# Shifted-window attention: the next pair's queries, keys and values projected ahead of a slot's transposes instead of behind its attention products

## The chip, the cores and the metric

One core of a Trainium2 chip runs the whole program. The metric is the device time of one execution in microseconds (us), lower is better. Engines are named as the profile names them: PE is TensorE (PEld its weight loads), ACT is ScalarE, DVE is VectorE, POOL is GpSimd.

## The reference

An input of 64 x 8192 goes through a convolution front end and then four residual blocks over 64 sequences of 128 positions with 64 channels. The change lies in the first block, attention inside windows of 128 positions. Here the sequence is exactly one window long, so it is plain attention with a position bias:

```python
h = h + _L0_attn_ref(_layernorm(h, axis=-1), qkv_weight, qkv_bias, proj_weight, proj_bias, bias_table)

qkv = xw @ qkv_weight.T + qkv_bias                 # 8 heads of 8 channels
attn = jnp.einsum('whqd,whkd->whqk', q * scale, k)
attn = attn + jnp.transpose(rpb, (2, 0, 1))[None]  # bias by relative position
attn = jax.nn.softmax(attn, axis=-1)
out = jnp.einsum('whqk,whkd->wqhd', attn, v).reshape(Bb * nW, WINDOW, C)
out = out @ proj_weight.T + proj_bias
```

All data is float32.

## The kernel before, in words

Each engine runs its own instruction stream, written out by hand, and semaphores join the streams. The stage of interest is the second (`stage2_pe`, `stage2_act`, `stage2_dve`, `stage2_pool`, lines 598 to 877). It works on pairs of sequences: two sequences of 64 channels fill the 128 partitions, which makes 32 pairs. A pair takes four **turns** (the code calls one `u`), each for four of its sixteen head-and-sequence combinations, so that one turn fills one PSUM bank of 128 x 512.

`pipelined` (line 580) calls `slot(i, t)` on every engine, with `i` from 0 to 16 and `t` from 0 to 7. Eight slots are two pairs: `l = t // 4` is the pair, `u = t % 4` the turn. Iterations 1 to 14 are a hardware loop on PE, ACT and DVE (on POOL from 2), the others are unrolled, and 16 is the tail. I call slot 4 of an iteration "slot 4", and a turn by the slot in which its scores are read.

A turn travels through the slots like this:

- Slot u = 0 of a pair: PE computes the scores of all four turns (L686, `scores`).
- Slot t: DVE adds the bias, and takes the extreme of each row (L836, four instructions), after which the scores are in SBUF.
- Slot t+1: ACT takes the exponential with a running sum (L787, four instructions of two records each).
- Slot t+2: DVE takes the reciprocal of the sums (L825), and POOL scales the weights (L620, `normed`).
- Slot t+3: PE transposes the weights into bank 4 (L738, four instructions). DVE (L845, even turns) or ACT (L792, odd turns) copies bank 4 to SBUF. There is one bank for it, so the next turn's transposes wait for that copy.
- Slot t+4: PE multiplies them by the values (L704, `attended`).

Around this, once for each pair:

- u = 0: PE transposes the next pair's normalised rows (L668, `rows`), ACT copies them (L767), PE projects the finished pair (L716, `project`) and DVE adds this to h (L858), which counts `a_h_r` up.
- u = 1: PE computes queries, keys and values of the next pair (L674, L675, L676, `qkv`), ACT copies the queries (L771) and DVE the keys (L818). `qkv` waits for the copied rows (L767) and for `a_h_r` of the projection in the slot just before (L858), since keys and projection share bank 3.
- u = 2: POOL spreads the keys over heads (L614, `spread`), which the next scores wait for.
- u = 3: PE runs `unread` (L691), one matmul of 128 x 512 whose result nobody reads, DVE copies the heads' outputs (L852), ACT the values (L777), and POOL prepares the next rows (L602, L606).
- Once in an iteration, at slot 5, DVE also sums and centres four finished sequences for the next layer norm (L275, L277).

The order within PE's slot is what the change touches. It was: scores, unread, the transposes L738, attended (not at u = 0), then `qkv` at u = 1.

Of the kernel before, what the change touches and what calls it, by code (L numbers as in the profile page):

```python
# [59 lines left out]
def build(nc, xp, consts, out):  # L60
# [8 lines left out]
    def c(name, a=0, b=None):  # L69

        o, w = ON[name]
        return cst[:, o + a:o + (w if b is None else b)]
# [263 lines left out]
    def bank(b):  # L336
        return T(b // 4, b % 4)
# [229 lines left out]
    N2 = NP // 2  # L567

    def back(i, t, d):

        return (i, t - d) if t >= d else (i - 1, t - d + 8)

    def i_is(i, k):
        return isinstance(i, int) and i == k

    def exists(i, d, last=N2 - 1):

        return not isinstance(i, int) or 0 <= i + d <= last

    def pipelined(engine, slot, ahead=1):  # L580

        for i in range(ahead):
            for t in range(8):
                slot(i, t)
        with engine.Fori(ahead, N2 - 1) as i:
            for t in range(8):
                slot(i, t)
        for t in range(8):
            slot(N2 - 1, t)
        for t in range(8):  # L590
            slot(N2, t)
# [3 lines left out]
    def scores_bank(t):  # L595
        return bank(SBANK[t % 4])
# [65 lines left out]
    def stage2_pe(pe, start=None):  # L662
        def rows(i, l):
            pe.wait_ge(a_xs_r, i * 2 + (l + 1))

            if l or exists(i, -1):
                pe.wait_ge(a_v_r, i * 2 + l)
            nc.tensor.transpose(bank(2)[:, 0:128], xs[l], eye).then_inc(a_t_r, 1)  # L668

        def qkv(i, l):  # L670
            pe.wait_ge(a_xT_r, i * 2 + (l + 1))

            pe.wait_ge(a_h_r, i * 2 + (l + 1))
            nc.tensor.matmul(bank(2)[:, 128:256], c("a_q"), xT[l], start=True, stop=True)  # L674
            nc.tensor.matmul(bank(3)[:, 0:128], c("a_k"), xT[l], start=True, stop=True)  # L675
            nc.tensor.matmul(bank(2)[:, 256:384], xT[l], c("a_v"), start=True, stop=True).then_inc(a_qkv_r, 1)  # L676

        def scores(i, l):

            pe.wait_ge(a_q_r, i * 2 + (l + 1))  # L680
            pe.wait_ge(a_kz_r, i * 2 + (l + 1))
            if l or exists(i, -1):
                pe.wait_ge(a_mx_r, i * 8 + 4 * l)
            for u in range(4):
                r = slice(32 * u, 32 * u + 32)
                nc.tensor.matmul(scores_bank(u), a_q[l][r, :], a_kz[l][r, :], start=True, stop=True).then_inc(a_sc_r, 1)  # L686

        def unread(i, l):

            pe.wait_ge(a_mx_r, i * 8 + (4 * l + 1))  # L690
            nc.tensor.matmul(scores_bank(0), eye, c("a_bias", 0, 512), start=True, stop=True)  # L691

        def attended(i, t):
            l, u = t // 4, t % 4
            if u % 2:
                pe.wait_ge(a_pta_r, i * 4 + (t // 2 + 1))
            else:
                pe.wait_ge(a_ptd_r, i * 4 + (t // 2 + 1))
            if u == 0:
                pe.wait_ge(a_v_r, i * 2 + (l + 1))  # L700

                pe.wait_ge(a_oT_r, i * 2 + (l + 2))
            for j in range(4):
                m = nc.tensor.matmul(bank(6)[32 * j:32 * j + 32, 128 * u:128 * u + 128], a_v[l][:, 128 * u + 32 * j:128 * u + 32 * j + 32],  # L704
                                     a_PT[t % 4][:, 128 * j:128 * j + 128], start=True, stop=True)
            m.then_inc(a_av_r, 1)

        def project(i, l):

            pe.wait_ge(a_oT_r, i * 2 + (l + 1))  # L710

            pe.wait_ge(a_h_r, i * 2 + (l + 1))
            for s in range(2):
                for g in range(2):
                    for half in (0, 64):
                        m = nc.tensor.matmul(bank(3)[half:half + 64, 128 + 64 * s:192 + 64 * s],  # L716
                                             a_oT[l][:, 128 * (2 * s + g) + half:128 * (2 * s + g) + half + 64], a_pp[:, 64 * g:64 * g + 64],
                                             start=(g == 0), stop=(g == 1))
            m.then_inc(a_pr_r, 1)

        def slot(i, t):
            l, u = t // 4, t % 4
            if i_is(i, 0) and t == 0:

                pe.wait_ge(b_h, ND)
            if u == 0 and exists(i, 0):
                scores(i, l)
            if u == 3 and exists(i, 0):
                unread(i, l)
            ib, tb = back(i, t, 3)  # L730
            if exists(ib, 0):
                pe.wait_ge(a_n_r, ib * 8 + (tb + 1))
                if tb % 2:
                    pe.wait_ge(a_ptd_r, ib * 4 + (tb // 2 + 1))
                elif tb or exists(ib, -1):
                    pe.wait_ge(a_pta_r, ib * 4 + tb // 2)
                for k in range(4):
                    m = nc.tensor.transpose(bank(4)[:, 128 * k:128 * (k + 1)], a_P[tb % 4][:, 128 * k:128 * (k + 1)], eye)  # L738
                m.then_inc(a_pt_r, 1)
            ib, tb = back(i, t, 4)  # L740
            if u and exists(ib, 0):
                attended(ib, tb)
            if u == 1 and exists(i, l, N2 - 1):
                qkv(i + l, 1 - l)
            if u == 0:
                if exists(i, l, N2 - 1):
                    rows(i + l, 1 - l)
                if exists(i, -1, N2 - 1):
                    project(i, l)
                if exists(ib, 0):  # L750
                    attended(ib, tb)
            if isinstance(i, int) and i == N2 and t < 2:
                stage3_pe(pe, start=t)
        if start == 0:
            rows(0, 0)
            return
        if start == 1:
            qkv(0, 0)
            return
        pe.wait_ge(f_dve, SETUP3)  # L760
        pe.wait_ge(m_loaded, LOADED7)
        pipelined(pe, slot)

    def stage2_act(act, start=None):
# [1551 lines left out]
```

## Time and profile before

| | |
|---|---|
| median of 3 runs | 1242.64 us (1241.76 to 1243.09) |
| profiled execution | 1241.4 us, its span 1239.5 us |
| stage 2 in the span | about 158 to 431 us |
| busy share of the span | PE 92%, DVE 69%, ACT 61%, POOL 50% |

Busy shares are means over stages with different limits. What a change in stage 2 is worth has to be read inside stage 2, and there in one iteration of its loop, since all iterations look alike. The end of a PE record is modelled; its start isn't. So PE's own pace is read from one start to the next. Each record of "x4" or "x8" is a merged line of the timeline: it gives the start of the first and the end of the last.

### The profile page before, as it was taken

What the parts mean: (1) busy time and instruction counts of PE and PEld (TensorE: products, weight loads), DVE (VectorE), ACT (ScalarE), POOL (GpSimd) and SP (SyncE); (2) the same over time, 40 slices, a digit from 0 to 9 for tenths busy, and PEclk for the clock granted to TensorE, in tenths of its full rate; (3) what the DMA queues carried; (4) which work ended last, traced back from release to release, by engine and by line L of the source; (5) the groups of instructions that cost most, each with busy time, mean ns of one, the idle gap of its engine ahead of it and who ended that gap; (6) DMA issues with size and microseconds to landing.
All of it is one profiled execution on the core that took longest, in us unless ns stands there. A gap on an engine that the chain in (4) does not pass through costs nothing.

```text
span 1239.5 us, 43739 instructions
## 1 busy us (share of the span) xinstructions
PE 1134.3 (92%) x16184; PEld 790.6 (64%) x16184; DVE 856.3 (69%) x3021; ACT 755.9 (61%) x2435; POOL 617.8 (50%) x939
## 2 busy tenths in 40 slices
PE   6989979999999889999999997999999999699997
PEld 3447745555555467777887786777777764367665
DVE  5965678888888767778878775555555556656664
ACT  0136779999999845555555554566666666454553
POOL 6012577777787634566555654333333332345445
PEclk9988999999999989999999998999999999799999
DMA  7000000000000000000000000000000000000000
GB/s 234 1 1 2 2 2 1 0 0 0 0 0 0 2 1 3 1 0 0 0 0 0 0 1 2 2 0 0 0 0 0 0 2 0 1 11 11 17 17 19
DMA packets 10834, 10.26 MB, mean 8 GB/s; under 512 B 9232, under 2 KB 9872, under 8 KB 10640
## 3 DMA queue, kind: packets, MB, share of 16 engines
q1 hardware_dynamic: 10768, 9.35, 2.5%
q8 instruction: 46, 0.75, 0.2%
q14 instruction: 20, 0.16, 0.0%
HBM read 7.25 MB, written 2.10 MB: 8 GB/s over the span
## 4 chain that ended last, share of the span: by engine, by line
PE 65%; POOL 12%; issue 11%; DVE 6%; ACT 5%; POOLq 1%; DMA 0%; SPq 0%; ACTq 0%; DVEq 0%
PE bank L1473 8%; POOL big L620 8%; PE bank L1821 5%; PE bank L1155 5%; PE bank L1839 5%; PE bank L1468 5%; PE bank L1144 3%; PE bank L1456 3%; PE bank L1233 3%; PE bank L159 3%; PE bank L1164 3%; PE bank L1182 2%; PE bank L1586 2%; PE bank L1223 2%; PE bank L1203 2%
## 5 line engine op out<-in xcount | busy, mean ns | idle before, releaser
L787 ACT ACTIVATE big<-big 128x128 f32<-128x128 f32 x512 | 199.2, 396 | 0.5 <-DVE big L836 0.5
L620 POOL TENSOR_TENSOR big<-big 128x512 f32<-128x512 f32 x128 | 133.0, 1039 | 59.9 <-DVE big L825 59.9
L1058 POOL TENSOR_TENSOR big<-big 128x512 f32<-128x512 f32 x64 | 65.6, 1045 | 128.6 <-DVE big L1332 128.6
L1554 POOL TENSOR_TENSOR big<-g_a,g_b 64x64 f32 x128 | 40.2, 314 | 171.7 <-DVE g_a L1544 171.7
L836 DVE CUSTOM_DVE_ANT_0 big<-bank,cst 128x128 f32<-128x128 f32 x512 | 117.9, 287 | 0.7
L1535 DVE TENSOR_TENSOR_SCAN g_t<-g_zero_r,bank 128x128 f32<-128x128 f32 x128 | 53.9, 421 | 86.9 <-ACT g_zero_r L1520 86.9
L738 PEld LDWEIGHTS bank<-cst,big 128*128 128x128 f32 x512 | 54.4, 141 | 83.8 <-POOL big L620 33.0
L738 PE MATMUL bank<-cst,big 128*128 128x128 f32 x512 | 83.0, 284 | 23.0 <-POOL big L620 13.2
L787 ACT ACTIVATION_READ_ACCUMULATOR big<-big 128x1 f32 x512 | 99.8, 195 | 0.0
L1742 POOL TENSOR_TENSOR big<-big 128x512 f32<-128x512 f32 x48 | 60.9, 1270 | 72.1 <-DVE big L1945 69.5
L1520 ACT ACTIVATE g_zero_r<-bank,g_bias 128x64 f32<-128x64 f32 x128 | 40.7, 318 | 89.9 <-PE bank L1473 89.8
L1875 ACT ACTIVATE big<-bank 128x512 f32<-128x512 f32 x128 | 66.0, 604 | 47.7 <-PE bank L1821 47.7
L1473 PEld LDWEIGHTS bank<-g_b,cst 128*64 128x64 f32 x1024 | 40.3, 136 | 57.3 <-DVE g_b L1542 57.0
L1155 PEld LDWEIGHTS bank<-big 128*128 128x128 f32 x512 | 61.2, 196 | 24.3 <-issue 23.5
L1839 PEld LDWEIGHTS bank<-cst,big 128*64 128x64 f32 x2048 | 62.5, 138 | 18.7 <-issue 17.4
L1473 PE MATMUL bank<-g_b,cst 128*64 128x64 f32 x1024 | 57.9, 234 | 10.2 <-DVE g_b L1542 10.0
L1278 ACT ACTIVATE big<-big 128x1024 f32<-128x1024 f32 x32 | 33.9, 1058 | 54.7 <-DVE big L1323 54.7
L1839 PE MATMUL bank<-cst,big 128*64 128x64 f32 x2048 | 66.8, 223 | 0.1
L1155 PE MATMUL bank<-big 128*128 128x96 f32 x512 | 66.5, 284 | 0.0
L1945 DVE TENSOR_TENSOR big<-bank,fB 128x512 f32<-128x512 f32 x64 | 44.3, 692 | 30.4 <-PE bank L1839 29.2
L1821 PE MATMUL bank<-big,cst 64*128 64x512 f32 x256 | 65.1, 624 | 0.0
L295 POOL TENSOR_TENSOR rstd<-eps_var,half_neg 128x4 f32 (+3 forms) x48 | 58.6, 1220 | 6.7 <-POOL eps_var L293 5.5
(271 smaller groups left out, 3100.3 us busy)
## 6 DMA issues: line engine op xcount, KB each, us to landing
cst<-consts_dram SPq DMA_DIRECT2D x1, 3364.5 KB, 14.1
out_dram<-h SPq DMA_DIRECT2D x8, 256.0 KB, 2.6
big<-x_dram SPq DMA_DIRECT2D x3, 512.0 KB, 5.7
cst<-consts_dram SPq DMA_DIRECT2D x3, 256.0 KB
big<-x_dram SPq DMA_DIRECT2D x1, 513.0 KB, 4.1
big<-consts_dram SPq DMA_DIRECT2D x4, 96.0 KB, 2.2
cst<-consts_dram SPq DMA_DIRECT2D x4, 48.0 KB, 1.9
g_ih_exchanged<-consts_dram SPq DMA_DIRECT2D x2, 96.0 KB, 7.9
```

Source lines behind the costliest of these rows:

```text
L620: nc.gpsimd.tensor_tensor(P, P, a_rs[t % 4].unsqueeze(2).to_broadcast([128, 4, 128]), ALU.mult).then_inc(a_n_r, 1)
L738: m = nc.tensor.transpose(bank(4)[:, 128 * k:128 * (k + 1)], a_P[tb % 4][:, 128 * k:128 * (k + 1)], eye)
L787: m = nc.scalar.activation(P, P, ACT.Exp, bias=a_mx[tb % 4][:, k:k + 1], scale=-1.0, accum_out=a_sm[tb % 4][:, k:k + 1])
L836: m = nc.vector.tensor_tensor_reduce(a_P[t % 4][:, 128 * k:128 * (k + 1)], scores_bank(t)[:, 128 * k:128 * (k + 1)], c("a_bias", 512 * (u ...
L1058: nc.gpsimd.tensor_tensor(w, w, f_rs[l][:, 8 * s:8 * s + 8].unsqueeze(2).to_broadcast([128, 8, 64]), ALU.mult).then_inc(f_w_r, 1)
L1155: m = nc.tensor.matmul(regions()[:, k // 4, k % 4, :], f_w[l][:, 128 * k:128 * k + 128], f_xs1[l][:, 96 * (k // 4):96 * (k // 4) + 96], st ...
L1468: nc.tensor.matmul(to[:, ::-1, 1, :] if s else to[:, :, 0, :], w, x, start=((half == 0 or gate == 2) and s == 0), stop=True, skip_group_ch ...
L1473: m = nc.tensor.matmul(to[64 * d:64 * d + 64, :], c("g_hh", 128 * gate + 64 * d, 128 * gate + 64 * d + 64), state[:, :], start=start, stop ...
L1742: nc.gpsimd.tensor_tensor(m_acc[l], m_ye[0] if e == 1 else m_acc[l], m_ye[e % 4], ALU.add).then_inc(m_acc_r, 1)
L1821: nc.tensor.matmul(hidden_bank(s, e), c("m_w1", 128 * e, 128 * e + 128)[64 * s:64 * s + 64], m_xT[l][64 * s:64 * s + 64, :], start=True, s ...
L1839: m = nc.tensor.matmul(out_bank(e)[64 * half:64 * half + 64, 64 * (2 * p + s):64 * (2 * p + s) + 64], hidden(e, s)[:, 128 * p + 64 * half: ...
L1875: nc.scalar.activation(hidden(e, s), hidden_bank(s, e), ACT.Relu).then_inc(m_ra, 1)
```

## The change

The call of `qkv` at the second turn (u = 1) moves in PE's stream. It stood behind the slot's transposes and attention products; now it stands ahead of both. No instruction is added or removed, and each keeps its waits.

```diff
@@ -727,6 +727,8 @@
                 scores(i, l)
             if u == 3 and exists(i, 0):
                 unread(i, l)
+            if u == 1 and exists(i, l, N2 - 1):
+                qkv(i + l, 1 - l)
             ib, tb = back(i, t, 3)
             if exists(ib, 0):
                 pe.wait_ge(a_n_r, ib * 8 + (tb + 1))
@@ -740,8 +742,6 @@
             ib, tb = back(i, t, 4)
             if u and exists(ib, 0):
                 attended(ib, tb)
-            if u == 1 and exists(i, l, N2 - 1):
-                qkv(i + l, 1 - l)
             if u == 0:
                 if exists(i, l, N2 - 1):
                     rows(i + l, 1 - l)
```

The transposes of line 738 are line 740 in the changed kernel. The streams of DVE, ACT and POOL are the same in both.

PE's stream in the loop, from the end of slot 4 over slot 5 to the transposes of slot 6, before. In the brackets, `2_h_written` is DVE's L858, `2_rowsT_copied` ACT's L767, `2_normed` POOL's L620, and `2_pT_copied_by_vector` and `..._by_scalar` the copies L845 and L792:

```order
L704 MATMUL bank<-big 32x128 [waits 2_heads_outT,2_v_ready,2_pT_copied_by_vector]
L704 MATMUL bank<-big 32x128 x3
L732 REGISTER_ALU
L738 MATMUL bank<-cst,big 128x128 [waits 2_pT_copied_by_scalar,2_normed]
L738 MATMUL bank<-cst,big 128x128 x3
L704 MATMUL bank<-big 32x128 [waits 2_pT_copied_by_scalar]
L704 MATMUL bank<-big 32x128 x3
L674 MATMUL bank<-big,cst 128x128 [waits 2_h_written,2_rowsT_copied]
L675 MATMUL bank<-big,cst 128x128
L676 MATMUL bank<-cst,big 128x128
L734 REGISTER_ALU [waits 2_normed]
L738 MATMUL bank<-cst,big 128x128 [waits 2_pT_copied_by_vector]
```

The same place now:

```order
L704 MATMUL bank<-big 32x128 [waits 2_heads_outT,2_v_ready,2_pT_copied_by_vector]
L704 MATMUL bank<-big 32x128 x3
L674 MATMUL bank<-big,cst 128x128 [waits 2_h_written,2_rowsT_copied]
L675 MATMUL bank<-big,cst 128x128
L676 MATMUL bank<-cst,big 128x128
L734 REGISTER_ALU
L740 MATMUL bank<-cst,big 128x128 [waits 2_pT_copied_by_scalar,2_normed]
L740 MATMUL bank<-cst,big 128x128 x3
L704 MATMUL bank<-big 32x128 [waits 2_pT_copied_by_scalar]
L704 MATMUL bank<-big 32x128 x3
L736 REGISTER_ALU [waits 2_normed]
L740 MATMUL bank<-cst,big 128x128 [waits 2_pT_copied_by_vector]
```

The wait for `2_h_written` now stands right behind slot 4's attention products. Between slot 5's transposes and slot 6's, which wait for DVE's copy of the former, only four attention products are left. Slot 1 and slot 2 change in the same way.

## Rows read from the trace of the kernel before

**Rows 1.** The page: its head, and busy time of each engine.

```profile
span 1239.5 us, 43739 instructions
...
PE 1134.3 (92%) x16184; PEld 790.6 (64%) x16184; DVE 856.3 (69%) x3021; ACT 755.9 (61%) x2435; POOL 617.8 (50%) x939
```

**Rows 2.** Busy time by stretch, one iteration and the stage: us, engines, PE's granted clock.

```profile
207.14:223.69 16.55, 15.22 (x165) 8.68 (x164) 14.14 (x94) 15.90 (x76) 12.87 (x16) 1.00 0.00 0
...
158.00:431.00 273.00, 245.19 (x2586) 139.41 (x2586) 228.49 (x1490) 255.66 (x1200) 210.46 (x261) 0.99 0.00 0
```

**Rows 3.** Groups by form, 207.14 to 422 us: busy us, mean ns, idle before.

```profile
L738 PE MATMUL bank<-cst,big 128*128 128x128 f32 x416 | 67.1, 283 | 15.3 <-POOL big L620 8.8 <-ACT big L792 5.8
...
L771 ACT ACTIVATE big<-bank,a_bqs 128x128 f32<-128x128 f32 x26 | 9.6, 367 | 8.4 <-PE bank L676 8.4
```

**Rows 4.** Timeline of ACT: start, duration, instruction, idle before it.

```profile
304.91 0.27 ACT L767 COPY big<-bank 128x128 f32<-128x128 f32 x1
...
307.05 0.37 ACT L771 ACTIVATE big<-bank,a_bqs 128x128 f32<-128x128 f32 x1 [0.32 <-PE bank L676]
...
312.88 0.57 ACT L792 COPY big<-bank 128x512 f32<-128x512 f32 x1
...
315.48 0.37 ACT L771 ACTIVATE big<-bank,a_bqs 128x128 f32<-128x128 f32 x1 [0.32 <-PE bank L676]
...
323.61 0.37 ACT L771 ACTIVATE big<-bank,a_bqs 128x128 f32<-128x128 f32 x1 [0.32 <-PE bank L676]
```

**Rows 5.** Timeline of DVE, the same iteration.

```profile
304.94 0.29 DVE L858 TENSOR_TENSOR h<-h,bank 128x128 f32 x1 [0.54 <-PE bank L716]
...
306.08 0.69 DVE L845 COPY big<-bank 128x512 f32<-128x512 f32 x1
307.05 0.35 DVE L818 TENSOR_SCALAR big<-bank,cst 128x128 f32<-128x128 f32 x1 [0.28 <-PE bank L676]
...
308.20 0.17 DVE L825 RECIPROCAL big<-big 128x4 f32<-128x4 f32 x1
...
313.44 0.29 DVE L858 TENSOR_TENSOR h<-h,bank 128x128 f32 x1 [0.47 <-PE bank L716]
...
321.49 0.29 DVE L858 TENSOR_TENSOR h<-h,bank 128x128 f32 x1 [0.54 <-PE bank L716]
```

**Rows 6.** Timeline of POOL, the same iteration.

```profile
308.45 1.04 POOL L620 TENSOR_TENSOR big<-big 128x512 f32<-128x512 f32 x1 [2.02 <-DVE big L825]
309.44 1.04 POOL L614 TENSOR_TENSOR big<-big,a_mask 128x512 f32<-128x512 f32 x1
```

**Rows 7.** Timeline of PE, the same iteration.

```profile
306.08 0.49 PE L674 MATMUL bank<-big,cst 128*128 128x128 f32 x2
...
306.85 0.63 PE L738 MATMUL bank<-cst,big 128*128 128x128 f32 x4
...
309.57 0.64 PE L738 MATMUL bank<-cst,big 128*128 128x128 f32 x4 [0.67 <-POOL big L620]
...
313.60 0.63 PE L738 MATMUL bank<-cst,big 128*128 128x128 f32 x4
...
317.91 0.66 PE L738 MATMUL bank<-cst,big 128*128 128x128 f32 x4 [0.43 <-ACT big L792]
```

**Rows 8.** Timelines of PE and of DVE in the last iterations, where no qkv is left.

```profile
422.59 0.63 PE L738 MATMUL bank<-cst,big 128*128 128x128 f32 x4 [0.59 <-DVE big L845]
...
423.51 1.13 PE L691 MATMUL bank<-cst 128*128 128x512 f32 x2
424.58 0.63 PE L738 MATMUL bank<-cst,big 128*128 128x128 f32 x4
...
426.08 0.63 PE L738 MATMUL bank<-cst,big 128*128 128x128 f32 x4 [0.52 <-DVE big L845]
...
425.24 0.69 DVE L845 COPY big<-bank 128x512 f32<-128x512 f32 x1
425.85 0.68 DVE L852 COPY big<-bank 128x512 f32<-128x512 f32 x1
```

## The prediction

> **What bounds the kernel now.** I read the views in this order: the page for the size of things, busy time by stretch for one iteration of the stage, groups for the waits that add up, then the four timelines over one iteration.
>
> The page names PE as the busiest engine, 92% of 1239.5 us [rows 1]. This is a mean over all stages, and it doesn't hold in the stage of the change. There one iteration (two pairs, eight slots) takes 16.55 us, and ACT is busy for 15.90 of them against PE's 15.22, DVE's 14.14 and POOL's 12.87 [rows 2]. The clock granted to PE is 1.00 in that iteration, the 2.4 GHz level, so it plays no part. The stage is 273 us long [rows 2].
>
> ACT is idle in one place only, in front of the copy of the queries, L771. The group shows 8.4 us before 26 of them, 0.32 us each [rows 3], always released by L676, the last of the three matmuls that move. The reader should see in the timeline of ACT that this comes twice in an iteration, at 307.05 and 315.48, and again at 323.61, which is 16.56 us after the first [rows 4]. So the stage runs at ACT's pace plus two waits for `qkv`, and the change goes straight for these waits. If nothing else were late, it would be a gain.
>
> PE is nearly as full, though. Over 104 slots (416 transposes) L738 waited 15.3 us in all [rows 3], of which I see two waits in an iteration: 0.67 us before 309.57 (slot 7, on POOL) and 0.43 us before 317.91 (slot 3, on ACT's copy) [rows 7]. That is all the slack that a later PE can use. So the question is how much later PE gets, and who waits for it.
>
> **The change, part by part.** Nothing is removed and nothing added, on any engine; no DMA is in it. What moves is one `qkv` per pair, for 31 of the 32 pairs (the first has its own ahead of the loop). It costs PE 0.77 us from its start to that of the next transposes (306.08 to 306.85) [rows 7].
>
> *The gain.* `qkv` would be done about a microsecond earlier for ACT. It can start once the rows' copy L767 is done (304.91 + 0.27 = 305.18) [rows 4] and once L858 is done (304.94 + 0.29 = 305.23) [rows 5]. The query copy started 0.97 us after L674 (306.08 to 307.05) [rows 4, 7], so it could start at 305.31 + 0.97 = 306.28. ACT is then still in its exponentials, and its 0.32 us of waiting goes. At most this is 31 x 0.32 = 9.9 us.
>
> *First loss, the wait for L858.* It was hidden, because `qkv` came 0.9 us behind it. Now it stands at the head of PE's slot. In slot 1 the transposes started at 313.60 [rows 7], before the end of L858 (313.44 + 0.29 = 313.73) [rows 5]. With 0.08 us to wake up (L845 ends at 306.77 [rows 5], and the transposes that it releases start at 306.85 [rows 7]), `qkv` starts at 313.81, and the transposes at 314.58 instead of 313.60: 0.98 us later.
>
> *Second loss, the cover of the copy.* The transposes of slot 2 need DVE's copy of slot 1's out of bank 4. `qkv` used to lie in that time and hid it. Now only four attention products do. The trace has this very case in its last iterations, where no `qkv` is left: transposes at 424.58, copy at 425.24, next transposes at 426.08, having waited 0.52 us [rows 8]. So from transposes to transposes it is 1.50 us, whatever PE has to do in between.
>
> *Slots 0 to 4.* From slot 2's transposes PE needs 0.92 us to `unread` (422.59 to 423.51) and 1.07 us from there to the next transposes (423.51 to 424.58) [rows 8]. So slot 3's transposes would start at 314.58 + 1.50 + 0.92 + 1.07 = 318.07. They started at 317.91 [rows 7]. The slack of 0.43 us is used up and 0.16 us is left over. From there PE runs without a wait to the projection and to L858. The step from one L858 to the next, 8.05 us before (313.44 to 321.49) [rows 5], becomes 8.21 us.
>
> *Slots 4 to 8.* Here the queue behind the wait matters. In slot 5 DVE's stream has the copy L845, then the keys L818, then the centring, and then the reciprocal L825 of turn 4, for which POOL, idle for 2.02 us, is waiting [rows 5, 6]. From the end of L858 at 305.23, with the same 0.08, the changed order gives: `qkv` 305.31, transposes 306.08, copy L845 0.66 us later (424.58 to 425.24) [rows 8] at 306.74, keys 0.61 us later (425.24 to 425.85, the next instruction behind a copy) [rows 8] at 307.35. They started at 307.05 [rows 5]: 0.30 us later, though their data is there sooner. All that follows keeps its distances: the centring and L825 at 308.20 [rows 5], POOL's L620 at 308.45 and the spreading of the keys right behind it at 309.44 [rows 6], slot 7's transposes, which waited for that L620 [rows 7], then scores, projection and L858 at 313.44 [rows 5]. I find no slack in this chain, so 8.50 us (304.94 to 313.44) become 8.80 us. ACT cannot keep its gain either: its exponentials of turns 6 and 2 need scores that DVE delivers from the same delayed queue.
>
> *The sum.* One iteration goes from 16.55 to 8.21 + 8.80 = 17.01 us, 0.46 us more. The chain turns 15 times (the projections begin in iteration 1, the last `qkv` is in slot 1 of iteration 15): 15 x 0.46 = 6.9 us. The tail behind the last `qkv` holds waits of PE for copies (0.59 and 0.52 us) [rows 8], which can take up about 0.5 us of the lag. That leaves +6.4 us. The profiled execution took 1241.4 us, so its counterpart would take 1247.8; against the median of 1242.64 it is **1249.0 us**.
>
> *Bounds.* The wake-up is the one size that repeats in every term. After an idle time it is 0.08 us (309.57 against POOL's end at 308.45 + 1.04) [rows 6, 7] and up to 0.15 us (426.08 against 425.24 + 0.69) [rows 8]. There are two such waits in each half, so 0.1 to 0.2 us more in an iteration if all take the longer one. On the other side the wait for L858 may fall into time in which PE is still issuing attention products; then slots 0 to 4 come out even, and only the 0.30 us remain. Low end 15 x 0.28 = 4.2, high end 15 x 0.7 = 10.5 us: 1246.8 to 1253.1.
>
> *A rule and the rows.* The row of ACT's waits [rows 3] and its 15.90 us of 16.55 [rows 2] say that ACT is the fullest engine and that its gap has one cause. The Trainium skill (Perfetto Trace Analysis, sections Identifying the Most-Contended Engine and Optimization Strategy) says to improve the engine with the highest occupancy first, by finding what its gaps wait for and making that start sooner. By this rule the change is right, and the sum would be the first rival's. The timelines of DVE and PE speak against it here.
>
> **The rivals.**
>
> *ACT stays the bound and its waits go* (faster). For it: 15.90 of 16.55 us busy, no other idle time. For this, PE's extra 0.16 and DVE's extra 0.30 us would have to be slack that I haven't seen, for instance if DVE's copy could go before the transposes' modelled end, or if POOL's chain had room. It decides from the point at which DVE's L818 starts no later than 307.05 in the frame of the iteration. Then the gain is up to 31 x 0.32 = 9.9 us, 1232.7 us; half of it, 1237.7, if only one half-iteration gains.
>
> *It comes out even* (no change). The lag in slots 5 to 8 costs 0.30 us, while in slots 1 to 4 PE keeps within its 0.43 us and ACT gains its 0.32 us there. Then the iteration stays at 16.55 within 0.02, and the time at 1242.6 us. For it: the miss in slots 1 to 4 is only 0.16 us, on sizes read to some hundredths. Against it: it needs both halves to differ, and the lag is handed on by L858 from one to the other.
>
> *More waits than the two that I price* (slower still). If slot 7's transposes and the scores of the next pair also slip against POOL, each turn of the chain could lose the 0.77 us that `qkv` takes on PE: 15 x 0.77 = 11.6 us, 1254.2 us.
>
> **How the numbers follow.** What a measurement of this kernel can tell from no change is about 0.2%, 2.5 us, so the borders are 1240.1 and 1245.1 us. My forecast has 0.68, the heavier loss 0.08, the even case 0.11, the faster one 0.13. So slower 0.76, same 0.11, faster 0.13. The range should leave out no more than 2 in 10: it takes the bounds of the forecast, the heavier loss and the upper part of the even case, 1242.0 to 1254.5 us, and leaves out the gain and some of the even case.
>
> **What would show each step.** In the profile of the changed kernel L771 should no longer wait on L676, and the idle time before it should be near nothing. ACT should wait instead for DVE's L836, 0.1 to 0.3 us, at turns 6 and 2, or for transposes before its copy L792. The transposes of slots 2 and 6 should wait on DVE's L845, about 0.5 us each. L674 should wait on L858, and L845 in slots 1 and 5 on the transposes. One iteration should take about 17.0 us, and stage 3 start 6 to 7 us later, with everything behind it unchanged. An iteration of 16.5 us or less would prove the chain through DVE wrong; one of 17.0 us with L771 still waiting would prove the first step wrong.

## The result, and the profile after

The changed kernel takes 1247.88 us (median of 8 runs, 1244.71 to 1249.41) against 1242.74 us (8 runs, 1241.3 to 1245.52): 5.1 us more, ratio 1.0038, 95% interval 1.0025 to 1.0051. Ratios are worked out over all executions, so they differ a little from the quotient of the medians. They leave out one execution of the kernel before that took 5529.4 us. Forecast were 1249.0 us, range 1242.0 to 1254.5, and slower. The profiled execution took 1246.27 us.

Busy time over one iteration, by stretch, changed kernel, columns as in [rows 2]:

```profile
306.25:323.15 16.90, 15.00 (x170) 8.71 (x162) 13.92 (x94) 16.30 (x76) 12.88 (x16) 1.00 0.00 0
```

16.90 us instead of 16.55 [rows 2], at the same granted clock. ACT's busy time has gone up from 15.90 to 16.30 us though it does the same work. An instruction that waits doesn't overlap the end of the one before it, and the profile counts the whole of both: ACT's L284 ends at 310.46 here and the exponentials that wait for DVE start at 310.87, while in the kernel before they start at 309.64, 0.10 us ahead of its end (309.32 + 0.42). A fuller bar isn't more work here.

Groups by form of the changed kernel, 207.14 to 422 us, those that answer to [rows 3] and those that now wait:

```profile
L787 ACT ACTIVATE big<-big 128x128 f32<-128x128 f32 x407 | 158.2, 393 | 5.4 <-DVE big L836 5.3
...
L740 PE MATMUL bank<-cst,big 128*128 128x128 f32 x408 | 65.2, 282 | 15.8 <-DVE big L845 12.3 <-POOL big L620 3.5
...
L845 DVE COPY big<-bank 128x512 f32<-128x512 f32 x52 | 36.0, 692 | 22.6 <-PE bank L740 21.6
...
L674 PE MATMUL bank<-big,cst 128*128 128x128 f32 x50 | 11.5, 311 | 6.4 <-DVE h L858 6.3
...
L771 ACT ACTIVATE big<-bank,a_bqs 128x128 f32<-128x128 f32 x25 | 9.1, 364 | 0.0
```

The wait before L771 is gone, all 8.4 us of it [rows 3]. In its place stand DVE's copy L845 waiting 22.6 us for the transposes, the transposes waiting 12.3 us for that copy, L674 waiting 6.3 us for L858, and ACT's exponentials waiting 5.3 us for DVE's bias and maximum.

One iteration on DVE, timeline, to be read beside [rows 5]:

```profile
306.25 0.29 DVE L858 TENSOR_TENSOR h<-h,bank 128x128 f32 x1 [0.54 <-PE bank L716]
...
308.07 0.69 DVE L845 COPY big<-bank 128x512 f32<-128x512 f32 x1 [0.59 <-PE bank L740]
308.68 0.34 DVE L818 TENSOR_SCALAR big<-bank,cst 128x128 f32<-128x128 f32 x1
...
309.81 0.17 DVE L825 RECIPROCAL big<-big 128x4 f32<-128x4 f32 x1
...
315.06 0.29 DVE L858 TENSOR_TENSOR h<-h,bank 128x128 f32 x1 [0.48 <-PE bank L716]
...
323.15 0.29 DVE L858 TENSOR_TENSOR h<-h,bank 128x128 f32 x1 [0.54 <-PE bank L716]
```

From L858 to the keys L818 it is 2.43 us instead of 2.11. From L858 to L858 it is 8.81 us over slots 4 to 8 (8.50 before) and 8.09 us over slots 0 to 4 (8.05 before).

The same iteration on PE, beside [rows 7] and [rows 8]:

```profile
307.43 0.60 PE L740 MATMUL bank<-cst,big 128*128 128x128 f32 x4
...
308.81 0.66 PE L740 MATMUL bank<-cst,big 128*128 128x128 f32 x4 [0.43 <-DVE big L845]
...
311.15 0.66 PE L740 MATMUL bank<-cst,big 128*128 128x128 f32 x4 [0.27 <-POOL big L620]
...
315.50 0.46 PE L674 MATMUL bank<-big,cst 128*128 128x128 f32 x2 [0.27 <-DVE h L858]
...
316.24 0.60 PE L740 MATMUL bank<-cst,big 128*128 128x128 f32 x4
...
317.71 0.66 PE L740 MATMUL bank<-cst,big 128*128 128x128 f32 x4 [0.52 <-DVE big L845]
...
318.66 1.13 PE L691 MATMUL bank<-cst 128*128 128x512 f32 x2
319.62 0.60 PE L740 MATMUL bank<-cst,big 128*128 128x128 f32 x4
```

The two losses stand in the brackets: L674 behind L858, and the next transposes behind the copy. The wait of slot 7 on POOL is down from 0.67 [rows 7] to 0.27 us, and that of slot 3 (0.43 us on ACT, [rows 7]) is gone. PE has spent most of its slack.

**How much of the 5.1 us lies in the stage.** I take the stage's length from the start of the last product of the stage before (L420) to that of the first transpose of stage 3 (L1136): 159.7 to 428.9, so 269.2 us before, and 159.4 to 432.3, so 272.9 us after. That is 3.7 us. The loop alone shows 4.5: thirteen iterations lie between the second L858 and the last in the loop, 189.10 to 404.24 us before and 187.98 to 407.62 after. The other 0.8 us is a gain that comes once, in iteration 1. ACT's L771 there, before:

```profile
183.09 0.37 ACT L771 ACTIVATE big<-bank,a_bqs 128x128 f32<-128x128 f32 x1 [1.84 <-PE bank L676]
```

It waited 1.84 us, since `qkv` stood behind transposes which themselves waited 1.47 us for POOL. With `qkv` ahead of them this first step, from one L858 to the next, went from 9.56 us (179.54 to 189.10) to 8.71 us (179.27 to 187.98). Of the kernels with one half of the change (below), the one with the early `qkv` in slot 1 takes 8.42 us for it, the other 9.36. The profiled span grew by 4.9 us (1239.5 to 1244.4), so 1.2 us of it lie in stages that the change doesn't touch; of the 5.1 us between the medians it would be 1.4. From the last L1136 to the end of the span it is 508.8 us before and 511.5 after, and in the kernels below between 507.5 and 512.6, on identical code. Stage 3 itself, from its first L1136 to its last, takes 299.7 to 303.5 us. So I read the effect of an edit from the iteration, and use the medians as a check.

### The profile page after: what moved, and what is told of

It is laid out like the page before. It is cut to its first block, busy times and chain, and to the rows that moved or that the text cites. A ratio compares the mean times of both kernels' runs of the same rounds, so it can differ in the third digit from the quotient of the medians.

```text
span 1244.4 us, 43739 instructions
## 1 busy us (share of the span) xinstructions
PE 1132.2 (91%) x16184; PEld 790.0 (63%) x16184; DVE 853.3 (69%) x3021; ACT 761.9 (61%) x2435; POOL 618.3 (50%) x939
## 4 chain that ended last, share of the span: by engine, by line
PE 65%; issue 12%; POOL 11%; DVE 6%; ACT 4%; POOLq 1%; DMA 0%; SPq 0%; ACTq 0%; DVEq 0%
PE bank L1473 8%; POOL big L620 6%; PE bank L1821 5%; PE bank L1155 5%; PE bank L1839 5%; PE bank L1468 5%; PE bank L1144 3%; PE bank L1456 3%; PE bank L1233 3%; PE bank L159 3%; PE bank L1164 2%; PE bank L1182 2%; PE bank L1586 2%; PE bank L1223 2%; PE bank L1203 2%
## 5 line engine op out<-in xcount | busy, mean ns | idle before, releaser
L787 ACT ACTIVATE big<-big 128x128 f32<-128x128 f32 x512 | 199.0, 394 | 6.3 <-DVE big L836 6.2
L620 POOL TENSOR_TENSOR big<-big 128x512 f32<-128x512 f32 x128 | 133.2, 1042 | 64.0 <-DVE big L825 64.0
L836 DVE CUSTOM_DVE_ANT_0 big<-bank,cst 128x128 f32<-128x128 f32 x512 | 117.8, 286 | 0.6
L740 PEld LDWEIGHTS bank<-cst,big 128*128 128x128 f32 x512 | 57.0, 141 | 77.8 <-DVE big L845 32.1
L740 PE MATMUL bank<-cst,big 128*128 128x128 f32 x512 | 82.3, 283 | 22.1 <-DVE big L845 15.5
L787 ACT ACTIVATION_READ_ACCUMULATOR big<-big 128x1 f32 x512 | 98.2, 192 | 0.0
L1821 PE MATMUL bank<-big,cst 64*128 64x512 f32 x256 | 67.7, 646 | 0.0
L845 DVE COPY big<-bank 128x512 f32<-128x512 f32 x64 | 44.3, 692 | 28.6 <-PE bank L740 27.4
```

The source lines that it names most:

```text
L620: nc.gpsimd.tensor_tensor(P, P, a_rs[t % 4].unsqueeze(2).to_broadcast([128, 4, 128]), ALU.mult).then_inc(a_n_r, 1)
L787: m = nc.scalar.activation(P, P, ACT.Exp, bias=a_mx[tb % 4][:, k:k + 1], scale=-1.0, accum_out=a_sm[tb % 4][:, k:k + 1])
L836: m = nc.vector.tensor_tensor_reduce(a_P[t % 4][:, 128 * k:128 * (k + 1)], scores_bank(t)[:, 128 * k:128 * (k + 1)], c("a_bias", 512 * (u ...
L1821: nc.tensor.matmul(hidden_bank(s, e), c("m_w1", 128 * e, 128 * e + 128)[64 * s:64 * s + 64], m_xT[l][64 * s:64 * s + 64, :], start=True, s ...
```

## The experiments

My theory: the lag has two parts. In slots 4 to 8 the later transposes hold up DVE's copy L845, and behind it in DVE's queue the keys, the centring and the reciprocal for which POOL waits. In slots 0 to 4 PE itself is on the chain, with the wait for L858 and the bare wait for the copy. The rivals are that all of it is the wait for L858, that all of it is DVE's queue, and that the pace isn't ACT's, so that no earlier `qkv` gains. "Stage" is the length as above. The iteration is one in the middle of the loop. The medians of the kernel before that ran beside each group were 1242.42, 1242.03 and 1242.77 us, and the ratios are to those runs.

| kernel | iteration us | slots 4 to 8 / 0 to 4 | stage us | median us | ratio to before, 95% |
|---|---|---|---|---|---|
| before | 16.55 | 8.50 / 8.05 | 269.2 | 1242.74 | 1 |
| the change | 16.90 | 8.81 / 8.09 | 272.9 | 1247.88 | 1.0038 (1.0025 to 1.0051) |
| early in slot 1 only | 16.50 | 8.42 / 8.08 | 267.3 | 1240.27 | 0.9975 (0.9958 to 0.9992) |
| early in slot 5 only | 16.82 | 8.81 / 8.01 | 273.0 | 1247.56 | 1.0030 (1.0012 to 1.0048) |
| change, keys first on DVE | 16.63 | 8.55 / 8.08 | 269.1 | 1243.08 | 0.9994 (0.9976 to 1.0011) |
| change, keys' product last | 16.32 | 8.51 / 7.81 | 264.8 | 1239.29 | 0.9972 (0.9954 to 0.9990) |
| both of these | 16.06 | 8.26 / 7.80 | 260.8 | 1235.99 | 0.9938 (0.9917 to 0.9960) |
| change, no unread matmul | 16.80 | 8.81 / 7.99 | 276.2 | 1247.10 | 1.0031 (1.0012 to 1.0051) |
| qkv in between | 15.94 | 8.13 / 7.81 | 259.7 | 1231.29 | 0.9912 (0.9883 to 0.9940) |
| the same again | 15.93 | 8.13 / 7.80 | 259.8 | 1233.83 | 0.9929 (0.9908 to 0.9950) |
| in between, keys apart | 15.94 | 8.14 / 7.80 | 259.3 | 1232.57 | 0.9921 (0.9902 to 0.9940) |
| in between, no unread | 15.92 | 8.13 / 7.79 | 259.5 | 1235.03 | 0.9930 (0.9904 to 0.9955) |

**One half of the change at a time.** In `slot` of `stage2_pe`, for slot 1 only:

```diff
-            if u == 1 and exists(i, l, N2 - 1):
+            if t == 1 and exists(i, l, N2 - 1):
                 qkv(i + l, 1 - l)
             ib, tb = back(i, t, 3)
...
                 attended(ib, tb)
+            if t == 5 and exists(i, l, N2 - 1):
+                qkv(i + l, 1 - l)
             if u == 0:
```

> qkv early in slot 1, late (as before) in slot 5. My theory (two losses, one in each half of the iteration, that hand on through L858): slots 4 to 8 take the 8.50 us of before, slots 0 to 4 the 8.09 of the changed kernel, so 16.6 us an iteration and a time within 1 us of before; L771 waits 0.3 us on L676 in slot 5 only. Rival A (the loss sits in the wait for L858 and comes with every early qkv): half of the changed kernel's loss, 16.7 us and 2.5 us over before. Rival B (ACT is the bound and every wait that goes is a gain): 16.2 us, 5 us faster than before.

Measured: 16.50 us, 8.42 and 8.08, ratio 0.9975. Slots 0 to 4 keep the changed kernel's time, and slots 4 to 8 not only fall back but below before: from L858 to the keys it is 2.03 us there (303.55 to 305.58) and 2.11 before, since `qkv` itself starts 1.06 us behind L858 instead of 1.14. L771 waits 0.54 us in slot 5, where 0.3 were expected. So the early `qkv` of slot 1 costs next to nothing by itself, and both rivals that give it a fixed price are out.

> qkv early in slot 5, late in slot 1. My theory: slots 4 to 8 take the 8.81 us of the changed kernel, because the copy L845 holds up keys, centring and the reciprocal on DVE; in slots 0 to 4 PE has its slack of 0.4 to 0.6 us again and can pay it back, as ACT is ahead: 16.3 to 16.6 us an iteration, -4 to +1 us against before. Rival A: 16.7 us, +2.5 us. If the chain through DVE were not the cause of the loss in slots 4 to 8, that part would take 8.5 us or less.

Measured: 16.82 us, 8.81 and 8.01, ratio 1.0030. The half of slots 4 to 8 is as expected, and it holds nearly all of the change's loss. The pay-back that I expected in slots 0 to 4 isn't there, and the 16.82 us lie outside my 16.3 to 16.6. ACT in that half, from the timeline of this kernel (its L773, L794, L860 and L740 are L771, L792, L858 and L738 of before):

```profile
301.23 0.37 ACT L773 ACTIVATE big<-bank,a_bqs 128x128 f32<-128x128 f32 x1 [0.57 <-PE bank L676]
...
303.03 0.56 ACT L794 COPY big<-bank 128x512 f32<-128x512 f32 x1
```

PE in the same stretch, from `qkv` to slot 3's transposes:

```profile
300.26 0.49 PE L674 MATMUL bank<-big,cst 128*128 128x128 f32 x2
...
303.65 0.66 PE L740 MATMUL bank<-cst,big 128*128 128x128 f32 x4 [0.40 <-ACT big L794]
```

PE's late start in slot 1 goes on to ACT through the queries (0.57 us of waiting), from there through the four exponentials to the copy, and from the copy back to PE. PE's 0.40 us of idle time looks like slack, but what ends it was made late by PE itself. This is also what [rows 7] shows at 317.91, and I had read it as slack.

**DVE's queue.** The changed kernel with the keys ahead of the copy in `slot` of `stage2_dve`:

```diff
+            if u == 1 and exists(i, l, N2 - 1):
+                keys(i + l, 1 - l)
             ib, tb = back(i, t, 3)
             if tb % 2 == 0 and exists(ib, 0):
...
-            if u == 1 and exists(i, l, N2 - 1):
-                keys(i + l, 1 - l)
```

> The changed kernel, and on DVE the keys L818 ahead of the copy L845. My theory: L818 fits into the 0.6 us in which DVE waits for the transposes, so the reciprocal of turn 4 comes 0.26 us earlier; slots 4 to 8 take 8.55 instead of 8.81 us, slots 0 to 4 stay at 8.09, 16.64 us an iteration, 4 us less than the changed kernel, 1 us over before. Rival A (only PE's wait for L858 counts): no change from the changed kernel, 16.9 us.

Measured: 16.63 us, 8.55 and 8.08, median 1243.08. An instruction that holds DVE for 0.26 us (308.68 to 308.94, start to start, in the changed kernel), moved into time in which DVE waits, takes 0.26 us off slots 4 to 8 and nothing off slots 0 to 4. DVE's queue carries the chain in the one and not in the other. The rival that counts only the wait for L858 falls.

**The wait for L858.** The changed kernel with the keys' product last, since it alone shares bank 3 with the projection:

```diff
             pe.wait_ge(a_xT_r, i * 2 + (l + 1))
-
-            pe.wait_ge(a_h_r, i * 2 + (l + 1))
             nc.tensor.matmul(bank(2)[:, 128:256], c("a_q"), xT[l], start=True, stop=True)
-            nc.tensor.matmul(bank(3)[:, 0:128], c("a_k"), xT[l], start=True, stop=True)
-            nc.tensor.matmul(bank(2)[:, 256:384], xT[l], c("a_v"), start=True, stop=True).then_inc(a_qkv_r, 1)
+            nc.tensor.matmul(bank(2)[:, 256:384], xT[l], c("a_v"), start=True, stop=True)
+            pe.wait_ge(a_h_r, i * 2 + (l + 1))
+            nc.tensor.matmul(bank(3)[:, 0:128], c("a_k"), xT[l], start=True, stop=True).then_inc(a_qkv_r, 1)
```

> The changed kernel with qkv's matmuls in the order queries, values, keys, and the wait for L858 only ahead of the keys, which alone share bank 3. My theory: that wait holds PE for 0.33 us in each half of the iteration (L674 could start at the end of the attention products), and PE is on the chain in both halves; so 8.48 and 7.76 us, 16.24 us an iteration, 10 us less than the changed kernel, about 1238 us. Rival D (only DVE's queue behind L845 counts, the wait for L858 is hidden by it): no change, 16.9 us.

Measured: 16.32 us, 8.51 and 7.81, stage 8.1 us shorter than the changed kernel's. The wait costs 0.30 and 0.28 us in the two halves, so it isn't hidden, and rival D falls.

> The same, and on DVE the keys L818 ahead of the copy L845. My theory: another 0.26 us less in slots 4 to 8 alone, 8.22 + 7.76 = 15.98 us an iteration, which is where ACT becomes the bound (15.94 with qkv between transposes and attention products): about 1234 us, still 2 to 3 us over that kernel. Rival D: as with the keys first alone, 16.64 us.

Measured: 16.06 us, 8.26 and 7.80. The two mends add up (0.25 us for the keys, as before). The two losses are in series in slots 4 to 8, which a single cause would not give.

**The unread matmul taken out of the changed kernel.** L691 is left out in slots 3 and 7; the outputs don't use it.

> The changed kernel without the unread matmul L691 in every slot 3 and 7 (its result is read nowhere). My theory: in slots 0 to 4 PE's work lies on the chain, so 0.54 us go there, until ACT's copy ends later than PE; in slots 4 to 8 nothing goes, as POOL's L620 holds the transposes of slot 7. 16.36 us an iteration, 8 us less than the changed kernel, if the granted clock stays at 1.00. Rival E: the clock falls to its lower level in the stage, and the kernel is slower than the changed one.

Measured: 16.80 us in an undisturbed iteration, 8.81 and 7.99. The 0 us of slots 4 to 8 is right, but in slots 0 to 4 only 0.10 of the 0.54 us goes. PE of this kernel in slot 3, timeline:

```profile
305.79 0.66 PE L740 MATMUL bank<-cst,big 128*128 128x128 f32 x4 [0.53 <-POOL big L620]
```

POOL ahead of it, whose L620 at 304.61 is the one waited for:

```profile
303.42 1.02 POOL L295 TENSOR_TENSOR rstd<-eps_var,half_neg 128x4 f32 x1 [0.17 <-POOL eps_var L293]
304.61 1.04 POOL L620 TENSOR_TENSOR big<-big 128x512 f32<-128x512 f32 x1 [0.17 <-DVE big L825]
```

POOL's scaling of turn 0 lets the transposes start only 0.10 us earlier than they do behind the unread matmul, and I had not followed that queue. The rest of the expectation, the clock, is half right. The median isn't higher than the changed kernel's, but the stage is 3.3 us longer, since in some places the granted clock falls. In the thirteen iterations of the loop slots 4 to 8 took 8.80 or 8.81 us nine times, and four times 9.94 to 10.31: 5.1 us lost, against 13 x 0.10 = 1.3 us that leaving the matmul out gives back. The loop's mean is 17.20 us an iteration (188.00 to 411.55), not 16.80. Three stretches of this kernel, busy time with the granted clock behind the engines:

```profile
200.00:220.00 20.00, 16.06 (x179) 9.21 (x178) 15.68 (x104) 18.46 (x85) 14.54 (x18) 0.91 0.00 0
220.00:240.00 20.00, 15.80 (x186) 9.38 (x182) 16.78 (x112) 19.50 (x92) 16.06 (x22) 1.00 0.00 0
...
340.00:360.00 20.00, 16.51 (x179) 9.46 (x178) 15.70 (x100) 18.63 (x87) 14.95 (x21) 0.91 0.00 0
```

Two executions of the same scores L686 in its timeline of PE:

```profile
212.76 2.09 PE L686 MATMUL bank<-big 32*128 32x512 f32 x8
...
298.88 1.14 PE L686 MATMUL bank<-big 32*128 32x512 f32 x8 [0.17 <-POOL big L614]
```

The first ran at a lower granted clock, 0.69 over 212.7 to 216 us, a mix of the two levels, 1.2 and 2.4 GHz; the second at 1.00. Before that fall PE had waited longer than in the kernel with the matmul (1.33 us on POOL ahead of 211.22, against 0.28 ahead of 209.78 there).

**The place in between.** If the losses are the wait for L858 and the bare copy, there is a place that has neither: behind the transposes, ahead of the attention products. The transposes and L845 should start when they did, L858 should have ended, and `qkv` should still cover the copy.

```diff
+            if u == 1 and exists(i, l, N2 - 1):
+                qkv(i + l, 1 - l)
             ib, tb = back(i, t, 4)
             if u and exists(ib, 0):
                 attended(ib, tb)
-            if u == 1 and exists(i, l, N2 - 1):
-                qkv(i + l, 1 - l)
```

> qkv behind the transposes and ahead of the attention products, in both halves. By my theory neither loss is there: the transposes and L845 start when they did before, L858 has ended by the time qkv starts, and qkv still covers the copy; queries and keys come 0.34 us earlier than before. ACT's wait before L771 falls from 0.32 us to under 0.1, an iteration takes 15.9 us, and the kernel 9 us less than before, about 1233.5 us. Rival C (any earlier qkv is lost to another wait, the stage's pace is not ACT's): 16.5 us, within 1 us of before.

Measured: 15.94 us, median 1231.29, ratio 0.9912 (0.9883 to 0.9940). Busy time of one of its iterations:

```profile
299.90:315.83 15.93, 15.11 (x166) 8.66 (x162) 13.96 (x93) 15.91 (x77) 12.85 (x17) 1.00 0.00 0
```

Its L771 in the timeline of ACT, with no bracket behind it any more, and the record ahead of it:

```profile
301.45 0.20 ACT L787 ACTIVATION_READ_ACCUMULATOR big<-big 128x1 f32 x1
301.66 0.37 ACT L771 ACTIVATE big<-bank,a_bqs 128x128 f32<-128x128 f32 x1
```

ACT is busy for 15.91 of 15.93 us. So the reading that ACT sets the pace and that its wait before L771 costs time was right: the gain of the first rival is there, 9.5 us in the stage (9.9 were its most). It only isn't to be had from the head of the slot. A little of the wait is left without showing: L771 starts 0.21 us behind the record ahead of it, where the next instruction elsewhere starts after 0.09 or 0.10. The copy isn't wholly covered either: slot 2's transposes wait 0.18 us for L845 (310.28). This version is faster than both kernels, and was so again in a second measurement:

> The kernel with qkv between transposes and attention products once more, beside the one with the split. My theory: 15.94 us an iteration again, and 10 to 11 us less than before; if the first measurement was a favourable chip, 8 us or less.

Measured: 15.93 us and 0.9929 (0.9908 to 0.9950). The median is 8.9 us under the 1242.77 of before, between the two expectations. The stage is 259.8 against 259.7 us, while the medians differ by 2.5 us. In the profiled executions, which differ by 2.3 us, that lies behind the stage, in stage 3 (303.1 against 300.6 us).

> qkv between transposes and attention products, its keys last with a semaphore of their own, so that ACT and DVE are each released by the matmul that they need. My theory: ACT is the bound, its wait before L771 (about 0.1 us twice an iteration) goes: 15.7 to 15.85 us an iteration instead of 15.94, 1 to 3 us less than the kernel without the split. Rival F (POOL's and DVE's chains hold the iteration at 15.9 by now): no change.

Measured: 15.94 us, 1232.57 us. The split gives nothing, so rival F stands. Its ACT timeline shows where the time went (L772, L788 and L837 are L771, L787 and L836 of before):

```profile
301.65 0.19 ACT L788 ACTIVATION_READ_ACCUMULATOR big<-big 128x1 f32 x1
301.75 0.36 ACT L772 ACTIVATE big<-bank,a_bqs 128x128 f32<-128x128 f32 x1
...
304.01 0.42 ACT L284 ACTIVATE squares<-xc 128x256 f32 x1
304.42 0.40 ACT L788 ACTIVATE big<-big 128x128 f32<-128x128 f32 x1
```

The hidden 0.11 us before L771 is gone (301.65 to 301.75). In its place the exponentials of turn 6 start 0.41 us behind L284, not 0.31 (303.94 to 304.25 without the split), and 0.03 us behind DVE's bias and maximum of that turn, whose last record (L837) starts at 304.31 and ends at 304.39. Another 0.11 us has come in behind the copy of the values (305.98 to 306.23, against 305.80 to 305.94); its releaser the views don't show. So the next thing in line is, in part, DVE's queue in slots 4 to 8. Which chain sets its pace I didn't isolate; slot 7's transposes wait 0.27 us on POOL in both kernels.

> qkv between transposes and attention products, and no unread matmul. My theory: ACT is the bound there (15.9 of 15.94 us), so PE's 0.96 us twice an iteration are worth nothing: 15.85 to 15.95 us, within 1.5 us of the kernel with it, if the granted clock stays. Rival E: the clock falls, and it is slower by more than 10 us.

Measured: 15.92 us in the loop, as expected, and 1235.03 us. The profiled span is 3.8 us longer than with the matmul. In the tail the clock falls earlier. Busy time by stretch, without the matmul:

```profile
410.00:420.00 10.00, 7.35 (x98) 4.81 (x95) 7.51 (x50) 9.01 (x42) 6.38 (x9) 0.86 0.01 2
```

The same stretch with it, in the kernel with `qkv` in between:

```profile
410.00:420.00 10.00, 7.59 (x99) 4.67 (x99) 7.54 (x49) 9.04 (x43) 6.50 (x9) 1.00 0.01 2
```

In the second measurement of that same kernel, matmul included, the granted clock was 0.95 over 410 to 420 us and 0.67 over 420 to 430. Over the latter stretch it was 0.67 without the matmul too, and 0.85 in the first measurement with it.

Stage 3's first L1136 starts at about the same time in the three profiles: 419.6 us without the matmul, 419.5 and 419.0 with it. Its last starts at 722.4, 720.1 and 722.1. The first L1144 takes 2.08, 1.13 and 1.90 us. So a slower clock at the start of stage 3 goes with a stage 3 that is some 2 us longer, but it came with the matmul too: that leaving the matmul out causes it isn't shown. The medians (1235.03, and 1231.29 or 1233.83) don't settle it either.

## Why the prediction was right

- **What bounds the stage, and the gain.** ACT's pace plus the wait before L771: right. The wait went entirely, and with `qkv` in between nearly all of it turned into a gain, 9.5 us.
- **First loss, the wait for L858.** Right in kind, too small in size: `qkv` starts 0.15 us behind the end of L858 (306.54 to 306.69, 315.35 to 315.50), not 0.08. The experiment with the keys' product last prices the whole wait at about 0.29 us in each half.
- **Second loss, the cover of the copy.** 1.50 us from transposes to transposes were forecast. It is 1.47 us in slot 1 (316.24 to 317.71) and 1.38 us in slot 5 (307.43 to 308.81). Right.
- **Slots 4 to 8.** 8.80 us forecast, 8.81 measured, by the chain as given: L845, keys, centring, L825, POOL. The run with the keys first shows it by 0.26 us for 0.26 us. Right.
- **Slots 0 to 4.** 8.21 us forecast, 8.09 measured. The step that failed is the 1.07 us from `unread` to the next transposes, taken from 423.51 to 424.58 in the tail [rows 8]. It is 0.96 us (318.66 to 319.62). Of the other steps, the way from there to L858 is 3.53 us (319.62 to 323.15) where 3.58 were kept from before, and the way from L858 to `unread` 3.60 (315.06 to 318.66) where the forecast has 3.56. The row in the tail carries no bracket, but POOL's scaling of that turn had started at 423.40 and takes 1.04 us, so the transposes could not have started before 424.44. So a wait seems to be hidden under PE's modelled end of the matmul before.
- **The slack of slot 3.** I called 0.43 us on ACT's copy slack that a later PE can use. The run with the early `qkv` in slot 5 only shows that it isn't, as long as `qkv` in slot 1 is late: ACT's copy follows PE's own `qkv`. In the changed kernel `qkv` is early in both, so the sum was not touched by it.
- **The sum.** 0.46 us an iteration forecast, 0.35 measured. For the stage 6.4 us were forecast and 3.7 measured: 13 x 0.35 = 4.5 in the loop, less 0.85 in iteration 1, where `qkv` no longer queues behind transposes that wait for POOL's long L295. That gain I hadn't looked for, because I read one iteration in the middle and multiplied. The 1249.0 us came nearer to the median's 1247.88 than the terms deserve, since some 1.4 us of the measured difference lie outside the stage. That part is luck.
- **Bounds.** Four waits an iteration at 0.07 us more each are 0.28 us, not 0.1 to 0.2; the high end of 0.7 us an iteration covers that. The low end is worked out with 0.28 us where the sentence before it has 0.30, which moves it by 0.3 us. The 0.35 us measured lie inside.
- **What should show.** L771 without a wait, ACT waiting for L836 at turn 6 (0.41 us at 310.87), the transposes waiting 0.43 and 0.52 us for L845, L674 for L858: all there, the one for L836 longer than the 0.1 to 0.3 us forecast. The same wait at turn 2 isn't: in that half the timeline shows none of the exponentials waiting on DVE. Stage 3 started 3.4 us later (428.9 to 432.3), not 6 to 7.

The rule that the engine with the highest occupancy comes first, and that one looks for what its gaps wait for (the Trainium skill, Perfetto Trace Analysis, sections Identifying the Most-Contended Engine and Optimization Strategy), named the right engine and the right gap. What this case adds with its numbers is that the place from which the gap is closed decides: 15.94 us an iteration from one, 16.90 from the other.

## What to carry to other kernels

Before moving work to the head of an in-order queue, ask which wait it covered where it stood: here `qkv` hid DVE's copy from PE, and the copy's delay stopped four DVE instructions that had nothing to do with it. Try the place just behind the instruction that others wait for; here it had nearly the whole gain and almost none of the loss. And idle time ahead of an engine is slack only if what ends it doesn't itself depend on that engine.

## What the runs showed of the hardware that was not expected

- The unread matmul L691 seems to keep the granted clock up in the changed kernel's loop. Without it the clock fell to 0.91 over 200 to 220 and over 340 to 360 us, one group of matmuls took 2.09 instead of 1.14 us, and the loop's mean rose from 16.90 to 17.20 us; that is one profiled execution, and in no profile of a kernel with the matmul did an iteration of the loop stretch like this. With `qkv` in between, leaving it out changed nothing in the loop (15.92 us an iteration), and at the start of stage 3 the clock fell with it and without it.
- PE started `qkv` 0.14 or 0.15 us behind the end of DVE's L858, but the transposes L740 0.05 or 0.06 us behind the end of DVE's copy L845 (308.76 to 308.81, 317.65 to 317.71). It had been idle ahead of both. In the tail before, it was 0.15 us behind the copy too (425.93 to 426.08). What makes the difference no run here shows.
- Stages that no edit touched differed by up to 5.1 us from one profiled execution to another (507.5 to 512.6 us from the last L1136 to the end), as much as the effect that was to be explained.
